# Self-attention's q and k round trip: loads of the second tile ahead of later stores, region rows in VectorE's gaps, the last four projections behind the first scores

## The reference

```python
qkv = hidden_states @ c_attn_w + c_attn_b            # 4 x 256 x 768
q, k, v = jnp.split(qkv, 3, axis=-1)                 # 16 heads of 16
scores = einsum('bhqd,bhkd->bhqk', q, k) / sqrt(16)
scores = where(causal, scores, mask_value)
attn = softmax(scores, axis=-1)
scaled = attn * mult[None, :, None, :]               # heads 0, 1, 2: 1.6 on one third of the keys each
scaled = scaled / sum(scaled, axis=-1, keepdims=True)
attn = where(div_heads, scaled, attn)
out = einsum('bhqk,bhkd->bhqd', attn, v) @ c_proj_w + c_proj_b
```

## Time and profile before

| | us |
|---|---|
| median of 3 runs | 674.49 |
| lowest and highest of the runs | 672.59, 676.24 |
| the profiled execution's own time | 672.18 |
| its span (first to last instruction) | 670.4 |
| mean granted clock of TensorE | 0.964 |

### The profile page before, as it was taken

One profiled execution on the slowest core, in us unless ns is written; L12 is line 12 of the kernel. 1 busy time (PEld: TensorE's weight loads), 2 busy tenths in 40 slices (PEclk: granted clock), 3 DMA queues, 4 the chain that ended last, 5 costly groups with the idle time before them and its releaser, 6 DMA issues. The chain is left out here.

```text
span 670.4 us, 10668 instructions
## 1 busy us (share of the span) xinstructions
PE 598.2 (89%) x3740; PEld 475.4 (71%) x3740; DVE 402.1 (60%) x794; ACT 348.1 (52%) x1047; POOL 249.6 (37%) x201
## 2 busy tenths in 40 slices
PE   5998999999999998997887867999999876769998
PEld 4887998899989987975555546555558652448887
DVE  3766566666667664336477777699995378335000
ACT  2545444444444435632787861579996366751210
POOL 1352262233223232022696770133546149155000
PEclk8999999999999999999797999999999996699999
DMA  7122012102211220019993000300006147680000
GB/s 258 64 95 94 32 65 94 64 32 82 77 65 36 93 77 0 2 58 171 196 204 127 0 1 4 124 0 0 1 1 137 51 127 236 202 254 8 17 17 23
DMA packets 41586, 53.48 MB, mean 80 GB/s; under 512 B 3649, under 2 KB 37057, under 8 KB 41409
## 3 DMA queue, kind: packets, MB, share of 16 engines
q1 hardware_dynamic: 41536, 52.84, 28.7%
HBM read 48.63 MB, written 4.19 MB: 79 GB/s over the span
## 5 line engine op out<-in xcount | busy, mean ns | idle before, releaser
L247 POOL TENSOR_TENSOR ctx_lo<-ctx_stage,ctx_hi 128x1024 fp32r<-128x1024 f32 x32 | 76.3, 2387 | 157.3 <-DVE ctx_hi L622 135.8
L637 DVE TENSOR_TENSOR pT_lo<-ps,pT_hi 128x512 fp32r<-128x512 f32 x64 | 41.2, 686 | 60.0 <-ACT pT_hi L517 60.0
L342 PE MATMUL ps<-ctx_hi,pT_hi 128*128 128x256 f32 x256 | 75.2, 294 | 1.5 <-DVE pT_lo L637 1.4
L343 PE MATMUL ps<-ctx_lo,pT_hi 128*128 128x256 f32 x256 | 72.4, 283 | 0.0
L344 PE MATMUL ps<-ctx_hi,pT_lo 128*128 128x256 f32 x256 | 72.4, 283 | 0.0
L494 ACT CAST ctxT_hi<-ps 128x512 fp32r<-128x512 f32 x64 | 34.6, 593 | 62.7 <-PE ps L299 62.5
L1688 ACT ACTIVATE comb<-comb,cneg 128x64 f32<-128x64 f32 x160 | 62.9, 401 | 0.0
L629 DVE TENSOR_SCALAR_CACHE_REDUCE scores<-ps,qbk 128x512 f32<-128x512 f32 x64 | 47.5, 750 | 21.2 <-PE ps L311 21.2
L1574 PE MATMUL pf<-phiT,h3T 128*128 128x512 f32 x128 | 60.2, 591 | 0.0
L1659 PE MATMUL pf<-phiT,comb 128*128 128x256 f32 x256 | 56.2, 379 | 0.0
L508 ACT ACTIVATE probs<-scores,negmax 128x512 f32<-128x512 f32 x64 | 46.0, 728 | 16.3 <-DVE rowsum L648 16.3
(11 more groups left out here) (204 smaller groups left out, 1368.3 us busy)
## 6 DMA issues: line engine op xcount, KB each, us to landing
ctx_stage<-in_ctx_dram SPq DMA_DIRECT2D x32, 512.0 KB, 3.3
w_more<-in_L_ffn_expert_w_dram SPq DMA_DIRECT2D x11, 1024.0 KB, 5.4
h3T<-in_L_ffn_expert_w_dram SPq DMA_DIRECT2D x5, 1024.0 KB, 5.3
qk_parts_dram<-qk_parts SPq DMA_DIRECT2D x8, 384.0 KB, 5.3
q_rows<-qk_parts_dram SPq DMA_DIRECT2D x24, 128.0 KB, 6.5
disp<-qk_parts_dram SPq DMA_DIRECT2D x24, 128.0 KB, 5.8
disp<-in_L_ffn_phi_w_dram SPq DMA_DIRECT2D x1, 2048.0 KB, 8.2
phiT<-in_L_ffn_expert_b_dram SPq DMA_DIRECT2D x4, 512.0 KB, 10.0
```

The source lines that it names most:

```text
L247: nc.gpsimd.tensor_tensor(ctx_lo[:, cols], ctx_in_sb[:, c % SLOTS, :], ctx_hi[:, cols].bitcast(F32), ALU.subtract).then_inc(split_g, 1)
L342: nc.tensor.matmul(pO[q][:, 0:D], pT_hi[:, c % 2, q, cols], hi, start=c == 0 and j == 0, stop=False)
L343: nc.tensor.matmul(pO[q][:, 0:D], pT_hi[:, c % 2, q, cols], lo, start=False, stop=False)
L637: nc.vector.tensor_tensor(pT_lo[:, c % 2, q, :], probs_banks(c, alone)[q][:], pT_hi[:, c % 2, q, :].bitcast(F32), ALU.subtract).then_inc(p ...
```

## The change

- SyncE's order becomes: stores 0 and 1, loads 0 and 1, stores 2 and 3, loads 2 and 3, and the same for 4 and 5, 6 and 7. The transfers are the same.
- `focus_rows` is cut in four. The factors (`focus_factor`) come before `rest_of(0)`, the memset of ones (`query_extras`) behind it, the memset of zeros (`key_extras`) behind `rest_of(1)`, and the regions (`key_focus`) behind `rest_of(3)`. The memset of ones writes pairs of bf16 as one float32.
- `QK_FIRST` becomes 4: stages 4 to 7 are all projected between the first scores, and ScalarE's and VectorE's parts of them stand between the exponentials and maxima of groups 0 and 1. GpSimd's `low_part(4)` and `low_part(5)` come behind `normalise(0, 0)`. `QK_BANK` gives stages 4 and 5 the banks 4 and 5. TensorE's first score no longer waits for `rest_v` 5 and 6 but for 3 and 4.

```diff
-            for s in range(8):
+            for s in range(0, 8, 2):
                 store_parts(s)
-                if s:
-                    stack_rows(s - 1)
-            stack_rows(7)
+                store_parts(s + 1)
+                stack_rows(s)
+                stack_rows(s + 1)
...
-        QK_FIRST = 6
+        QK_FIRST = 4
-        QK_BANK = (4, 5, 0, 1, 0, 1, 6, 7)
+        QK_BANK = (4, 5, 0, 1, 4, 5, 6, 7)
... TensorE
-            for s in range(4, QK_FIRST):
-                pe.wait_ge(rest_v, s - 1)
-                project_qk(s)
             pe.wait_ge(consts_g, 2)
             pe.wait_ge(frows_v, 5)
             for s in range(2):
                 pe.wait_ge(rows_in[s], 16 * STACK)
             for part in range(2):
-                pe.wait_ge(rest_v, QK_FIRST - 1 + part)
+                pe.wait_ge(rest_v, 3 + part)
                 score(0, 0, part)
             score(0, 0, 2)
+            pe.wait_ge(values_v, 3)
+            project_qk(4)
             pe.wait_ge(xadd_v, QT)
             score(0, 1, 0)
-            for s in range(QK_FIRST, 8):
-                pe.wait_ge(values_v, s - QK_FIRST + 1)
-                project_qk(s)
             pe.wait_ge(values_v, 4)
+            project_qk(5)
             score(0, 1, 1)
+            project_qk(6)
             score(0, 1, 2)
+            project_qk(7)
... ScalarE: stages 4 and 5 no longer ahead of exps(0, 0, *)
             for part in range(3):
                 exps(0, 0, part)
+            high_part(4)
+            middle_part(4)
+            exps(0, 1, 0)
+            high_part(5)
+            middle_part(5)
+            exps(0, 1, 1)
             high_part(6)
             middle_part(6)
-            exps(0, 1, 0)
+            exps(0, 1, 2)
             high_part(7)
             middle_part(7)
-            exps(0, 1, 1)
-            exps(0, 1, 2)
             exps(0, 2, 0)
... VectorE
+            def query_extras():
+                nc.vector.memset(q_rows[extra, 0:FOCUSED, :].bitcast(F32), TWO_ONES).then_inc(frows_v, 1)
+            def key_extras():
+                nc.vector.memset(k_rows[extra, 0:FOCUSED, :], 0.0).then_inc(frows_v, 1)
             last_attended()
+            focus_factor()
             rest_of(0)
+            query_extras()
             rest_of(1)
+            key_extras()
             last_sums()
             rest_of(2)
             last_norm()
             rest_of(3)
-            for s in range(3):
+            key_focus()
+            for s in range(4):
                 values(s)
-            focus_rows()
-            values(3)
-            for s in range(4, QK_FIRST):
-                rest_of(s)
             for part in range(3):
                 maxima(0, 0, part)
             invert_sums(0, 0, 0)
+            rest_of(4)
             maxima(0, 1, 0)
-            rest_of(6)
             invert_sums(0, 0, 1)
-            rest_of(7)
+            rest_of(5)
             maxima(0, 1, 1)
             invert_sums(0, 1, 0)
+            rest_of(6)
             maxima(0, 1, 2)
+            rest_of(7)
             invert_sums(0, 1, 1)
             maxima(0, 2, 0)
```

More of the change, by code:

```diff
@@ L2 @@
 import math
+import struct
 from contextlib import ExitStack
@@ L797, in self_attention @@
     RING = 4
+    TWO_ONES = struct.unpack("<f", struct.pack("<I", 0x3F803F80))[0]
     with ExitStack() as st:
@@ L1168, in _ @@
             nc.scalar.copy(hT[:, :, LAST * S:B * S], split_halves(bank[2][:])).then_inc(h2T_a, 1)
-            for s in range(4, QK_FIRST):
-                high_part(s)
-                middle_part(s)
             def exps(b, g, part):
@@ L1260, in values, with focus_factor @@
                                         b_v[:].unsqueeze(1).broadcast_to([P, 2, D]), ALU.add).then_inc(values_v, 1)
[L1262 to L1265, removed]
+            extra = slice(ROWS, ROWS + NPART)
+            def focus_factor():
                 for r, part in enumerate(focus_parts):
@@ L1273, in focus_rows, with key_focus @@
                         nc.vector.tensor_scalar(focus[extra, :], unit, part, None, ALU.mult).then_inc(focus_v, 1)
+            def query_extras():
+                nc.vector.memset(q_rows[extra, 0:FOCUSED, :].bitcast(F32), TWO_ONES).then_inc(frows_v, 1)
+            def key_extras():
+                nc.vector.memset(k_rows[extra, 0:FOCUSED, :], 0.0).then_inc(frows_v, 1)
+            def key_focus():
                 dve.wait_ge(focus_v, NPART)
```

## The result

The changed kernel takes 683.68 us (median of 6 runs, 681.95 to 685.85), against 673.98 for the kernel before in as many runs. The medians differ by 9.7 us. The ratio of the two sets of runs is 1.0137, 95% interval 1.0106 to 1.0169, which is slower by 9.2 us. I had forecast 675.9, with 671.0 to 680.5 as the range, so the time lies outside it, on the slow side. The profiled execution has a span of 680.2 us (before 670.4).

The account below looks back on a forecast made before the run. The landing of `phi_b`, behind SyncE's full DMA queue, was taken to bound batch 0. Lead of scores 0, region rows 0, drains and rate +1.4, on the runs' median 674.49, gave 675.9 us, range 671.0 to 680.5.

Parts of the forecast that it names:

- What bounds the kernel: End of batch 0: the time goes by the landing of `phi_b`, set by amount of DMA work, rate and gaps.
- The gate: End of batch 0, where VectorE idles 1.32 us until `phi_b` lands, then casts it while ScalarE and TensorE wait.
- Drains and rate: DMA queue running dry at loads 2, 4 and 6 (1.2 us in all), then slower row loads: +1.4 us together.
- the dip: Lower DMA share in loads 3 of the kernel before, 0.96 instead of 1.15, worth 0.8 us.
- the rate falls back in full: Slower rival: three drains empty all 16 DMA engines, loads restart in step; +2.8 to +6.7, 677.3 to 681.2 us; chance 0.26.
- SyncE's order, first pair: Loads 1 issued at about 302.4 instead of 304.60, bytes done at 311.4 instead of 312.9 us, gaining about 1.5 us.
- Region rows at a cost of 0 to 0.1: `focus_rows` pieces in VectorE's gaps fit into waits of 1 to 2 us; the memset of ones delays `rest_of(1)` some 0.1.
- Stages 4 to 7 behind the first scores: First score 3.6 us earlier, but GpSimd's third parts end at about 330.5 us; VectorE reaches `phi_b`'s cast at 348 to 350.
- The clock: TensorE's granted clock drops again after idling, under four projections instead of two: up to 2 x 1.8 us, hidden behind ScalarE.
- The gate opens earlier: Faster rival: two load groups side by side mix better than one behind a store; -3.5, 671.0 us; chance 0.10.

## Why the prediction was wrong, point by point

**What bounds the kernel: right.** The gate was the place, it stayed the place, and its shift is the result: +10.8 us at the landing, -1.6 from the shorter cast, +9.2 at the maxima, and 9.8 in the spans, against 9.7 by the medians. The stretch from the cast to the end, which I had said would keep its 319.1 us, took 318.2, with the cast 1.6 us shorter in it.

**Drains and rate: the step that failed, by its size.** I had put "+1.4 us", half of the 2.8 that a fall to the pace after the dip would cost. It measured +10.8: by the bytes, loads 2 to 7 take 10.5 us more, of which 3.9 - 0.8 = 3.1 are the drains and 7.4 the rate, and loads 1 take 1.3 more. Loads 0 begin 0.5 later; stores 2 to 7 take 0.9 less, and `phi_b` with its landing 0.6 less. The drains were named in the forecast as what slows the rate ("each drain puts the engines in step again"). That is half of the mechanism: the other half, that two groups with no store between slow each other without any drain (loads 1: 6.2 us), is not in it. Three choices made the term small. The dip that I took as the model of a drain had a share of 0.96 over its group and of 0.43 at its lowest, so it had not emptied the engines; in the new drain at loads 2 it fell to 0.04. "The new drains are shorter than the dip" was a guess: at 1.0 to 1.5 us each they lost more than the dip's 0.8. The engines stood empty for about the 0.4 us that I had said, but they also lost time running out and filling up, as the half microseconds above show. And I let the groups of a pair follow each other at "5.4 + 4.9", where the 4.9 was measured behind a store; without the store it is 6.2. (What the forecast calls "loads `s - 2`" in the queue are loads `s - 1`: store `s` is followed by them. The count of what stays in the queue is right.)

**The rival "the rate falls back in full": right in kind, too small in range** (677.3 to 681.2). Its far end was built from the same 4.9. With the 6.2 us that a group directly behind another took it would have had 3 x (5.4 + 6.2) + 1.2 = 36.0 for loads 2 to 7, and a time of 685. The Trainium skill's 109 GB/s, which I had set beside it, overstates the loss: by its 7.2 us a group the gate moves by 17.8 us, against the 10.8 measured.

**SyncE's order, first pair: right on the issue, wrong on the landing.** Loads 1 went out at 302.84 (302.4 forecast), but their bytes were done at 313.2, not 311.4. The first score came at 315.16 (312 to 313.5 forecast, 316.19 before):

```profile
315.16 0.58 PE L1032 MATMUL ps<-disp,q_rows 99*128 99x128 bf16 x4 [4.33 <-DMA disp<-qk_parts_dram]
```

**Region rows at a cost of 0 to 0.1, and no gain: both wrong.** The memset of ones took its 1.34 us, but began late and did not fit. The rest of stage 1 behind it came 0.5 us later, first before, then after:

```profile
296.22 0.75 DVE L1233 SCALAR_TENSOR_TENSOR qk_rest<-ps,b_qk,qk_parts 128x512 f32<-128x512 f32 x1 [1.28 <-ACT qk_parts L1148]
```

```profile
295.33 1.34 DVE L1277 MEMSET q_rows<- 3x1536 f32 x1 [0.38 <-issue]
296.70 0.75 DVE L1234 SCALAR_TENSOR_TENSOR qk_rest<-ps,b_qk,qk_parts 128x512 f32<-128x512 f32 x1
```

So store 1 and loads 0 came 0.5 us later too, which is a small part of the loss. And by the run with them alone the region rows are worth 5.9 us, because stages 4 and 5 stood behind them and through store 4 the whole queue. In the change this gain does not appear, since stages 4 and 5 are moved behind the first scores at the same time. No kernel has that move alone. With the region rows it costs 8.5 us of the stretch, and the region rows alone gave 6.6, so if the two add up it costs some 15 by itself (an estimate).

**Stages 4 to 7 behind the first scores: "GpSimd is what eats the lead", right and too mild.** GpSimd's last third part ended at 333.7 instead of 330.5, and VectorE came to the gate at 351.6 (before 349.9), not at 348 to 350. In the old order the lateness alone costs 8.5 us. In the new one it lies under the slow loads.

**The clock.** The drop came as forecast: the granted clock was 0.50, the level of 1.2 GHz, around the first scores, after TensorE had stood for 4.33 us. Of the four projections only the first was slower (3.52 us against 1.88). Behind them TensorE stood for 2.54 us until 329.57, where the score comes that needs row loads 2 and 3.

**The gate opens earlier: excluded.** That two groups side by side "mix better than a group behind a store" is the reverse of what was measured.

## What to carry to other kernels

Where a DMA queue is full, its rate is a term of the sum like any other: transfers into 16 partitions ran at 125 to 138 GB/s next to their like, and at over 200 with wide transfers between and no gap. Before narrow loads are put next to each other, or a store is taken from between them, look at GB/s by group and not only at the busy share, which was 1.15 in both cases. And find the last transfer of a queue that some engine waits for; every delay ahead of it is paid there, as every idle gap in VectorE ahead of an early store was paid here.

## What the runs showed of the hardware

A DMA share of 1.15 went with anything from 126 to 205 GB/s for the same 1 KB pieces from the same DRAM rows; loads into 32 or 64 partitions moved 223 GB/s at a share of 0.76. So the busy share did not tell the rate.

The cast of `phi_b` (96 x 2048, float32 to bf16, SBUF to SBUF) took 1.22 to 1.24 us alone, 2.78 in the kernel before, and 4.13 in the kernel with `phi_b` between store 3 and loads 2. There GpSimd worked through its whole start:

```profile
353.16 1.04 POOL L934 TENSOR_TENSOR eA<-eA,rinv 128x512 f32<-128x512 f32 x1
354.15 1.90 POOL L937 TENSOR_TENSOR eB<-eB,rinv 128x1024 f32<-128x1024 f32 x1
```

```profile
353.00 4.13 DVE L1345 CAST phib<-disp 96x2048 bf16<-96x2048 f32 x1
```

GpSimd ended at 356.05, the cast 1.1 us later, about its own length. In the kernel before GpSimd had begun a normalising at 351.06, just ahead of the cast, and the cast ended 1.1 us after it too. With the region rows alone the cast came first, and GpSimd's next normalising took 2.01 us instead of 1.04. The Trainium skill (SBUF — State Buffer, on who interferes with whom) describes a pair of ports that VectorE in a two-port mode and GpSimd hold one at a time for a whole instruction; these durations agree with it.
